# The offsets' convolution in products of one width: 27 products of 32 columns on four strips

## The chip, the cores and the metric

The kernel runs on one core of a Trainium2 chip. The time is that of the device from start to end of the program, in microseconds (us), as the median of several runs. A profile is one execution recorded by the hardware; its span is the time from the first to the last instruction of the program.

## What is computed

The input x is 2 images of 128 channels and 128 x 128 pixels. Two layers are added to it in turn. The first (a gated product with 128 x 128 weights, over group-normalized x) is done before the part that is changed here. The second is a deformable convolution over x after a group norm and a relu: an ordinary 3 x 3 convolution gives 18 offsets per pixel, two for each of nine taps; each tap then samples the image at its own shifted, fractional position, and the nine samples are multiplied by the weights.

```python
x = jax.nn.relu(x)                                   # of the normalized x
offset = conv3x3(x, w_off) + b_off                   # 128 -> 18 channels
py = base_y + off[:, :, 0]                           # off: [image, tap, 2, row, column]
px = base_x + off[:, :, 1]
samp = _bilinear_gather(x, py, px)                   # 128 channels, 9 taps, each pixel
out = jnp.einsum('bckhw,ock->bohw', samp, w_def)     # added to x
```

## The kernel before

All is written out by hand: each engine has its own list of instructions, and semaphores tie them. The first layer fills roughly the first fifth of the span. Then the second runs over 64 bands, each 8 rows by 64 columns of pixels (two sides of 16 row blocks of two images). `bands` (L447) walks a fixed list, `ORDER` (L425), once per band, and each engine does from it the steps that it has. Each step has a lead: in one pass, the offsets of band n + 3 (`O`, `Q`, `h`), the windows `z` of band n + 2, the weights `k` and the transposes `T` of band n + 1, the sampling steps `s0` to `s15` of band n and the nine taps `c0` to `c8` of the last convolution of band n - 1 are done. The part of the list that matters: `h0 s0 s1 s2 k0 h1 c0 c1 s3 s4 T0 k1 z0 z1 O0 s5 s6 P0 k2 c2 c3 s7 s8 T1`.

The pixels that the offsets' convolution reads are split in two float16 numbers. ScalarE makes `z_near` (`cast_z`, L1043: norm and relu from `raw`, a ring of 44 rows; where the rows of a band cross the ring's end this takes two instructions) and casts it to the high part `z_hi` (L1031). VectorE subtracts the two to get the low part `z_lo` (`split_z`, L1392). The weights are split as well: `woff` holds for each tap 32 columns of high part (`woff_hi`) and beside them 32 of low part (`woff_lo`), 18 of each 32 in use.

The step `O0` on TensorE is `offsets` (L901): it waits for `z_hi` and runs `convolve_offset_parts` (L887), which writes one PSUM bank of 128 partitions by 512 pixels. First come nine products of `z_hi`, one for each tap, with the 64 columns of both weight parts, in turn to partitions 0 to 63 and 64 to 127 (L895). Then a wait for `z_lo`, and nine products of `z_lo` with the 32 columns of `woff_hi`, in turn to partitions 64, 0, 96 and 32. What lies in the four strips of 32 partitions is added later, by the `select` matrix. Then ScalarE evicts the bank (`evict_offsets`, L1054).

Around it: ahead of the block TensorE transposes windows (`T0`, L867) and behind it come the sampling matmuls (`s5`, L851), whose results ScalarE (L1070) and VectorE (L1382) copy out of PSUM. GpSimd multiplies the hats into sampling weights, six pieces per band (`weigh`, L1666); the first waits until sampling step 15 of the band before is done. The products of the last convolution are L816, those that place the hats L831 and L834. L765 is a matmul of the first layer.

Of the kernel before, what the change touches and what calls it, by code (L numbers as in the profile page):

```python
# [12 lines left out]
TAPS, NOFF = 9, 18  # L13
# [5 lines left out]
BR, WC, UW = 8, 4, 64  # L19
# [88 lines left out]
def preact_conv_kernel(nc, x, Wa, ba, Wb, bb, Wg, bg, Wo, bo, w_off, b_off, w_def,  # L108
                       ident_d, group_mask_d, select_d, select_all_d, coords_d, out):
    with ExitStack() as ctx:  # L110
        def sb(name, shape, dt=F32):
            return ctx.enter_context(nc.sbuf_tensor(name, shape, dt))
# [15 lines left out]
        bank = [pairs[0][:, 0], pairs[0][:, 1], pairs[1][:, 0], pairs[1][:, 1]]  # L128
# [27 lines left out]
        woff = sb("woff", [P, TAPS, 2 * 32], F16)  # L156
        woff_hi, woff_lo = woff[:, :, 0:32], woff[:, :, 32:2 * 32]
# [56 lines left out]
        z_hi, z_lo = (sb(n, [P, UW + 2, BR + 2], F16) for n in ("z_hi", "z_lo"))  # L214
# [182 lines left out]
        B_OFF, B_CONV, B_ZT, B_S = 0, 2, 3, (4, 5, 6, 7)  # L397
# [286 lines left out]
        def _(pe):  # L684
# [49 lines left out]
            for j in range(3):  # L734
# [6 lines left out]
                             stop=True).then_inc(abg, 1)  # L741
            pe.wait_ge(abg, ABG_STEPS)

            def group(g, s):
# [48 lines left out]
                elif known and g == 6:  # L793
# [11 lines left out]
                             stop=True).then_inc(final, 1)  # L805
            pe.wait_ge(final, 4)
            nc.tensor.matmul(bank[B_ST][:, 2 * GROUPS:3 * GROUPS], average[:], devs2[:],
                             start=True, stop=True).then_inc(final, 1)
# [77 lines left out]

            def convolve_offset_parts(n):  # L887

                products = [(z_hi, k, 2 * 32, k % 2 * 64) for k in range(TAPS)]
                products += [(z_lo, k, 32, (64, 0, 96, 32)[k % 4]) for k in range(TAPS)]  # L890
                for i, (pixels, k, width, at) in enumerate(products):
                    if i == TAPS:
                        pe.wait_ge(z_lo_ready, n + 1)
                    ky, kx = k // 3, k % 3
                    mm = nc.tensor.matmul(  # L895
                        bank[B_OFF][at:at + width, :].rearrange("p (w r) -> p w r", r=BR),
                        woff[:, k, 0:width], pixels[:, kx:kx + UW, ky:ky + BR],
                        start=(i < 2), stop=(i + 4 >= len(products)), tile_position=(0, at))
                return mm

            def offsets(n, u, _):  # L901
                pe.wait_ge(z_hi_ready, n + 1)
                wait(pe, dist_ready, n)
                convolve_offset_parts(n).then_inc(off_done, 1)
# [816 lines left out]
```

## Time and profile before

| | |
|---|---|
| median of 3 runs | 1606.08 us (1605.52 to 1608.66) |
| the profiled execution | 1607.68 us |
| its span | 1605.9 us |
| TensorE busy | 1521.9 us |
| VectorE, ScalarE, GpSimd busy | 1064.8, 1005.7, 909.4 us |
| L895, products of `z_hi`: number, mean | 576, 412 ns |

Busy time is the union of an engine's instructions. Matmuls overlap in the array: a recorded matmul of 512 columns lasts some 380 ns while the next one starts 215 ns after it, so starts say more than durations. PE is TensorE's matmul, PEld its weight load, DVE VectorE, ACT ScalarE, POOL GpSimd. The clock is the share of full speed that was granted.

### The profile page before, as it was taken

Reading aid. Unit: us, or ns where it says so; the run is one execution under the profiler, and the core shown is the slowest. Engines: PE = TensorE matmul, PEld = TensorE weight load, DVE = VectorE, ACT = ScalarE, POOL = GpSimd, SP = SyncE. Lnnn points to the kernel's source line nnn. Section 1 sums busy time; section 2 is a strip of 40 time slices with the busy share of each in tenths; the row PEclk is TensorE's granted clock in tenths of the full one; section 3 lists DMA queues with packets and bytes.
Section 4 is the critical chain, followed back from the end, with each engine's and each line's share of the span. In section 5 each row is a group of like instructions: output and inputs, shape, how many; then the busy total and the mean of one; then the engine's idle time right before and its main releaser. Section 6 shows DMA issues by size and latency. Waiting matters only on the chain.

```text
span 1605.9 us, 27017 instructions
## 1 busy us (share of the span) xinstructions
PE 1521.9 (95%) x8915; PEld 993.1 (62%) x8916; DVE 1064.8 (66%) x2154; ACT 1005.7 (63%) x1820; POOL 909.4 (57%) x563
## 2 busy tenths in 40 slices
PE   5999999955999999999999999999999999999998
PEld 4777777733666566656666666665666665666664
DVE  4888888754566666666666666666666666666664
ACT  2555555535667676667666676666666676666663
POOL 3555555615566566655556666555556665655561
PEclk9999999968999999999999999999999999999999
DMA  4334333335676666666666666666666666666550
GB/s 138 106 115 120 109 110 119 90 115 166 182 214 197 184 195 187 192 189 182 191 189 184 184 189 188 197 193 191 185 185 196 194 192 182 188 193 185 172 161 27
DMA packets 190705, 268.05 MB, mean 167 GB/s; under 512 B 19810, under 2 KB 128382, under 8 KB 190590
## 3 DMA queue, kind: packets, MB, share of 16 engines
q1 hardware_dynamic: 190590, 266.60, 56.7%
q8 instruction: 61, 1.00, 0.3%
q14 instruction: 54, 0.44, 0.1%
HBM read 188.33 MB, written 78.18 MB: 166 GB/s over the span
## 4 chain that ended last, share of the span: by engine, by line
PE 73%; issue 11%; POOL 6%; SPq 3%; DVE 3%; ACT 2%; DMA 1%; POOLq 0%; ACTq 0%; DVEq 0%
PE bank L851 31%; PE pair L816 22%; PE pair L895 7%; PE pair L867 7%; POOL samples_hi L1612 4%; PE pair L831 2%; PE pair L834 2%; DVE z_lo L1392 2%; POOL rstd L1566 1%; DMA hat_x<-hats 1%; POOL samples_lo L1578 1%; ACT samples_hi L1070 1%; ACT abg_space L1043 1%; SPq L622 1%; PE bank L724 1%
## 5 line engine op out<-in xcount | busy, mean ns | idle before, releaser
L1666 POOL TENSOR_TENSOR weights<-hy_all,hx_all 112x768 f32<-112x768 f32 x384 | 723.0, 1918 | 510.6 <-PE bank L851 467.1
L1382 DVE SCALAR_TENSOR_TENSOR samples_lo<-bank,samples_hi 128x288 f16<-128x288 f32 (+1 forms) x1024 | 455.1, 464 | 351.0 <-ACT samples_hi L1070 343.5
L1070 ACT ACTIVATE samples_hi<-bank 128x288 f16<-128x288 f32 (+1 forms) x1024 | 402.2, 420 | 328.9 <-PE bank L851 308.0
L851 PE MATMUL bank<-weights,zT 112*128 112x288 f32 (+1 forms) x2176 | 598.2, 404 | 0.0
L851 PEld LDWEIGHTS bank<-weights,zT 112*128 112x128 f32 x2176 | 381.7, 191 | 131.8 <-issue 36.7
L816 PE MATMUL pair<-samples_hi,w_hi 128*128 128x512 f16 x576 | 219.0, 380 | 1.3 <-DVE samples_lo L1382 1.3
L816 PE MATMUL pair<-samples_lo,w_hi 128*128 128x512 f16 x576 | 217.5, 378 | 0.0
L816 PE MATMUL pair<-samples_hi,w_lo 128*128 128x512 f16 x576 | 217.4, 377 | 0.0
L867 PE MATMUL pair<-ident,z 128*112 128x128 f32 x1088 | 171.7, 273 | 10.4 <-DVE zT L1402 9.0
L867 PEld LDWEIGHTS pair<-ident,z 128*112 128x112 f32 x1088 | 132.4, 133 | 66.4 <-DVE zT L1402 9.9
L972 ACT ACTIVATE samples_hi<-pair,nbias,rstd 128x512 f32<-128x512 f32 x64 | 49.7, 777 | 155.0 <-PE pair L715 94.7
L1578 POOL TENSOR_TENSOR samples_lo<-samples_hi,samples_lo 128x512 f16<-128x512 f32 x64 | 74.1, 1157 | 126.1 <-ACT samples_lo L981 126.0
L1020 ACT ACTIVATE z<-raw,norm_band 128x1904 f32<-128x1904 f32 (+3 forms) x80 | 131.0, 1658 | 0.0
L1080 ACT COPY zT<-pair 112x512 f32<-112x512 f32 (+1 forms) x192 | 91.9, 479 | 37.3 <-PE pair L867 33.2
L1043 ACT ACTIVATE abg_space<-raw,norm_band 128x660 f32<-128x660 f32 (+2 forms) x74 | 104.1, 1420 | 12.2 <-DMA raw<-x_pad 12.2
L895 PE MATMUL pair<-z_hi,woff 128*64 128x512 f16 x576 | 87.3, 412 | 13.0 <-ACT z_hi L1031 13.0
L816 PEld LDWEIGHTS pair<-samples_lo,w_hi 128*128 128x128 f16 x576 | 55.3, 96 | 69.5 <-issue 0.3
L1367 DVE TENSOR_SCALAR hats<-dist 128x1024 f32<-128x1024 f32 x64 | 44.8, 700 | 80.3 <-ACT dist L1063 69.4
L1402 DVE COPY zT<-pair 112x512 f32<-112x512 f32 x128 | 87.8, 686 | 11.7 <-PE pair L867 11.7
L816 PEld LDWEIGHTS pair<-samples_hi,w_lo 128*128 128x128 f16 x576 | 56.5, 98 | 60.3 <-issue 0.3
L816 PEld LDWEIGHTS pair<-samples_hi,w_hi 128*128 128x128 f16 x576 | 55.8, 97 | 59.5 <-DVE samples_lo L1382 17.8
L1063 ACT ACTIVATE dist<-pair 128x1024 f32<-128x1024 f32 x64 | 65.5, 1023 | 37.4 <-PE pair L834 37.4
(141 smaller groups left out, 1762.9 us busy)
## 6 DMA issues: line engine op xcount, KB each, us to landing
hy_all<-hat_y SPq DMA_DIRECT2D x384, 192.0 KB
hx_all<-hat_x SPq DMA_DIRECT2D x384, 192.0 KB
hat_y<-hats SPq DMA_DIRECT2D x256, 126.0 KB
raw<-x_pad SPq DMA_DIRECT2D x68, 272.0 KB, 4.4
x_pad<-hy_all SPq DMA_DIRECT2D x64, 272.0 KB, 3.3
weights<-in_x SPq DMA_DIRECT2D x64, 256.0 KB, 3.0
out<-y SPq DMA_DIRECT2D x32, 512.0 KB, 3.6
hat_x<-hats SPq DMA_DIRECT2D x128, 72.0 KB
```

The costliest lines, as they stand in the source:

```text
L816: mm = nc.tensor.matmul(bank[B_CONV].rearrange("p (h c) -> p h c", h=2), w_part[:, k, :], part[:, u, k::TAPS, k % 3 * HR:k % 3 * HR + HALF ...
L851: mm = nc.tensor.matmul(sampled_step(n, p)[:, :, c0 - first:c1 - first], zT[0:WPIX, u * WINDOWS + w, :], weights[0:WPIX, u, :, c0:c1], sta ...
L867: mm = nc.tensor.transpose(bank[B_ZT][0:WPIX, (w % 4) * P:(w % 4 + 1) * P], z[:, u, w].rearrange("p r c -> p (r c)"), ident[:])
L895: mm = nc.tensor.matmul(bank[B_OFF][at:at + width, :].rearrange("p (w r) -> p w r", r=BR), woff[:, k, 0:width], pixels[:, kx:kx + UW, ky:k ...
L1020: done = nc.scalar.activation(z[:, u, :, rows, :], patches, ACT.Relu, bias=norm_band[:, 1].rearrange("p b n -> p (b n)")[:, n:n + 1], scal ...
L1043: done = nc.scalar.activation(z_near[:, :, r0:r1], raw[:, src:src + r1 - r0, left:left + UW + 2].rearrange("p r w -> p w r"), ACT.Relu, bi ...
L1070: nc.scalar.activation(samples_hi[:, u, :, c0:c1], sampled_step(n, p), ACT.Copy).then_inc(samples_ready, 1)
L1080: nc.scalar.copy(zT[0:WPIX, at:at + c, :].rearrange("p w c -> p (w c)"), bank[B_ZT][0:WPIX, 0:c * P]).then_inc(zT_a, 1)
L1382: nc.vector.scalar_tensor_tensor(out=samples_lo[:, u, :, c0:c1], in0=sampled_step(n, p), scalar=1.0, in1=samples_hi[:, u, :, c0:c1], op0=A ...
L1402: nc.vector.tensor_copy(zT[0:WPIX, at:at + c, :].rearrange("p w c -> p (w c)"), bank[B_ZT][0:WPIX, 0:c * P]).then_inc(zT_v, 1)
L1578: nc.gpsimd.tensor_tensor(xT_lo[:], xT[:], xT_hi[:], ALU.subtract).then_inc(xT_lo_ready, 1)
L1666: nc.gpsimd.tensor_tensor(to, hy_all[0:WPIX, i * TROWS:(i + 1) * TROWS, :], hx_all[0:WPIX, i * TROWS:(i + 1) * TROWS, :], ALU.mult).then_i ...
```

## The change

The offsets' convolution is done as three passes over the nine taps: `z_hi` with `woff_hi`, `z_hi` with `woff_lo`, `z_lo` with `woff_hi`. All 27 products have 32 columns, and product i writes the strip of 32 partitions that begins at 32 (i mod 4). The wait for `z_lo` stands ahead of the nineteenth product instead of the tenth. Nothing else is changed.

```diff
             def convolve_offset_parts(n):
 
-                products = [(z_hi, k, 2 * 32, k % 2 * 64) for k in range(TAPS)]
-                products += [(z_lo, k, 32, (64, 0, 96, 32)[k % 4]) for k in range(TAPS)]
-                for i, (pixels, k, width, at) in enumerate(products):
-                    if i == TAPS:
+                q = 4
+                for i in range(3 * TAPS):
+                    if i == 2 * TAPS:
                         pe.wait_ge(z_lo_ready, n + 1)
+                    k, at = i % TAPS, i % q * 32
+                    pixels, w = ((z_hi, woff_hi), (z_hi, woff_lo), (z_lo, woff_hi))[i // TAPS]
                     ky, kx = k // 3, k % 3
                     mm = nc.tensor.matmul(
-                        bank[B_OFF][at:at + width, :].rearrange("p (w r) -> p w r", r=BR),
-                        woff[:, k, 0:width], pixels[:, kx:kx + UW, ky:ky + BR],
-                        start=(i < 2), stop=(i + 4 >= len(products)), tile_position=(0, at))
+                        bank[B_OFF][at:at + 32, :].rearrange("p (w r) -> p w r", r=BR),
+                        w[:, k, :], pixels[:, kx:kx + UW, ky:ky + BR],
+                        start=(i < q), stop=(i + q >= 3 * TAPS), tile_position=(0, at))
                 return mm
```

## Rows read from the trace of the kernel before

**Rows 1.** The page: engine, busy us, share of the span, number of instructions.

```profile
PE 1521.9 (95%) x8915; PEld 993.1 (62%) x8916; DVE 1064.8 (66%) x2154; ACT 1005.7 (63%) x1820; POOL 909.4 (57%) x563
```

**Rows 2.** Windows: length, busy PE, PEld, DVE, ACT, POOL, clock, DMA share, GB/s.

```profile
750.83:769.72 18.89, 18.89 (x102) 11.61 (x101) 11.98 (x25) 13.13 (x26) 11.35 (x7) 1.00 0.70 200
1092.13:1111.95 19.82, 19.19 (x101) 11.60 (x101) 13.57 (x25) 13.42 (x26) 11.31 (x7) 1.00 0.61 178
```

**Rows 3.** Timeline, an ordinary band: start, us, engine, line, operation, count, idle time before.

```profile
1016.35 1.32 PE L895 MATMUL pair<-z_hi,woff 128*64 128x512 f16 x9
...
1018.41 0.75 PE L851 MATMUL bank<-weights,zT 112*128 112x288 f32 x2
```

**Rows 4.** Waits: engine and line, releaser, us in total, times, longest.

```profile
PEld pair L895 <- DVE z_lo L1392: 17.0, 12, 4.6
```

**Rows 5.** Windows of L895 alone, band 1: length, busy PE, PEld, clock, DMA, GB/s.

```profile
358.00:361.00 3.00, 2.56 (x13) 0.83 (x17) 0.50 0.39 113
```

**Rows 6.** Timeline of PE in narrow windows of the block in rows 3.

```profile
1016.81 0.49 PE L895 MATMUL pair<-z_hi,woff 128*64 128x512 f16 x2
...
1017.08 0.59 PE L895 MATMUL pair<-z_hi,woff 128*64 128x512 f16 x3
...
1017.30 0.38 PE L895 MATMUL pair<-z_hi,woff 128*64 128x512 f16 x1
1017.60 0.45 PE L895 MATMUL pair<-z_lo,woff 128*32 128x512 f16 x4
...
1017.83 0.44 PE L895 MATMUL pair<-z_lo,woff 128*32 128x512 f16 x4
...
1018.10 0.38 PE L895 MATMUL pair<-z_lo,woff 128*32 128x512 f16 x1
```

**Rows 7.** Groups by line, windows holding products 3-5 and 6-8: count, busy, mean ns.

```profile
L895 PE MATMUL pair<-z_hi,woff 128*64 128x512 f16 x3 | 0.7, 432 | 0.0
...
L895 PE MATMUL pair<-z_hi,woff 128*64 128x512 f16 x3 | 0.6, 378 | 0.0
```

**Rows 8.** Timeline of VectorE in the band of rows 3.

```profile
1015.89 0.84 DVE L1392 TENSOR_TENSOR z_lo<-abg_space,z_hi 128x660 f16<-128x660 f32 x1
```

**Rows 9.** Timeline of PE in the first layer.

```profile
201.06 0.83 PE L765 MATMUL pair<-abg_space,samples_lo 128*128 128x128 f16 x12
201.73 0.38 PE L768 MATMUL pair<-samples_lo,abg_space 128*128 128x512 f16 x1
```

**Rows 10.** Timeline of PE in a band that waits for `z_lo`.

```profile
1092.13 1.32 PE L895 MATMUL pair<-z_hi,woff 128*64 128x512 f16 x9
1094.08 0.88 PE L895 MATMUL pair<-z_lo,woff 128*32 128x512 f16 x9 [0.63 <-DVE z_lo L1392]
1094.89 0.51 PE L851 MATMUL bank<-weights,zT 112*128 112x288 f32 x1
```

**Rows 11.** Timeline of ScalarE behind the block in rows 3.

```profile
1021.47 0.90 ACT L1070 ACTIVATE samples_hi<-bank 128x288 f16<-128x288 f32 x2 [1.37 <-PE bank L851]
```

**Rows 12.** Timeline of PEld and PE ahead of the block in rows 3.

```profile
1015.58 0.60 PEld L867 LDWEIGHTS pair<-ident,z 128*112 128x112 f32 x4
...
1015.82 0.60 PE L867 MATMUL pair<-ident,z 128*112 128x128 f32 x4
```

**Rows 13.** Timeline of PEld from 1017.59 to 1017.82.

```profile
1017.60 0.12 PEld L895 LDWEIGHTS pair<-z_lo,woff 128*32 128x32 f16 x8 [0.41 <-issue]
```

**Rows 14.** Timeline of GpSimd, first and third piece; third piece and `z_lo` when waiting.

```profile
1012.41 1.82 POOL L1666 TENSOR_TENSOR weights<-hy_all,hx_all 112x768 f32<-112x768 f32 x1 [7.54 <-PE bank L851]
...
1015.96 2.47 POOL L1666 TENSOR_TENSOR weights<-hy_all,hx_all 112x768 f32<-112x768 f32 x1
...
1091.51 1.82 POOL L1666 TENSOR_TENSOR weights<-hy_all,hx_all 112x768 f32<-112x768 f32 x1
...
1091.68 2.35 DVE L1392 TENSOR_TENSOR z_lo<-abg_space,z_hi 128x660 f16<-128x660 f32 x1
```

**Rows 15.** Timeline of ScalarE, copy of sampling step 15 in the band of rows 3.

```profile
1012.29 0.53 ACT L1070 ACTIVATE samples_hi<-bank 128x432 f16<-128x432 f32 x1 [0.47 <-PE bank L851]
```

## Prediction

> **What bounds the kernel now.** I read the page first, then the kernel band by band, then one band product by product. The page gives TensorE 95% of the span [rows 1]. Windows over whole bands are sharper: an ordinary band lasts 18.89 us and TensorE is busy for all of it, while ScalarE has 13.13, VectorE 11.98 and GpSimd 11.35; a slow band lasts 19.82 with 19.19 of TensorE [rows 2]. So a microsecond taken out of the offsets' convolution (L895) in an ordinary band comes off the span, as long as no other engine turns into the wait.
>
> The block of L895 begins at 1016.35 in the band I chose, and the sampling matmul behind it at 1018.41: 2.06 us [rows 3]. The list of waits says that 12 of the 64 bands wait there for `z_lo` [rows 4]; bands 1 and 2 stand in the opening chain, before the clock has risen for good (0.50 in the stretch of the first of them [rows 5]). That leaves 64 - 12 - 2 = 50 ordinary bands, and the sum is made for these.
>
> **What a product costs.** Narrow windows show single starts. Of the products of 64 columns two run at once: tap 4 starts at 1016.81, tap 6 at 1017.08, tap 8, the ninth, at 1017.30. Of those of 32 columns four start together at 1017.60, four at 1017.83, and the ninth at 1018.10 [rows 6]. Two products on the same columns are thus 0.215 or 0.27 apart, and which of the two it is follows the tap: products 3 to 5 of the nine last 432 ns in the trace and the last three 378 [rows 7], so taps 3 to 5 (those with ky = 1) take 54 ns more than the others. The first product of a strip has its weight load ahead of it: 0.23 to the second. At the end of each half the array runs empty: tap 8 would be done at 1017.30 + 0.215, and the narrow half starts at 1017.60, 0.09 later; behind the last narrow one it is from 1018.10 + 0.215 to 1018.41, again 0.095. Two checks: taps 0 and 2 ahead of tap 4 take 1016.81 - 1016.35 = 0.46, twice 0.215 and a load; and in the narrow half tap 0 and tap 4 ahead of tap 8 take 0.23 + 0.27 = 0.50, the rows' 1018.10 - 1017.60. I use this rule for the change.
>
> **The change, part by part.** *Width.* Nine products of 64 columns, two at a time, become eighteen of 32, four at a time: as much array time, and nine weight loads and nine matmuls more per band. *Strips.* Product i goes to strip i mod 4. Strip 1 has the longest queue, taps 1, 5, 0, 4, 8, 3, 7: its seventh product starts at 0.23 + 0.27 + 0.215 + 0.27 + 0.215 + 0.27 = 1.47 and ends at 1.685. The last product of all, strip 2's seventh, follows it in order and ends with it. *One width.* The emptying in the middle goes, the one at the end stays: 1.685 + 0.095 = 1.78. Half columns that stood idle are filled as well: the ninth wide product ran beside nothing. Against 2.06 this is 0.28 less. *The wait.* It stands at the nineteenth product, which the rule puts at 0.985 after the block's start, 1017.34. `z_lo` is done at 1015.89 + 0.84 = 1016.73 [rows 8], so the wait is met 0.6 us early. Behind it on TensorE queue nine products, the sampling steps 5 and 6 and all that follows. *The extra instructions.* 27 pairs of load and matmul come to 1.47/26 = 56 ns each. L765 has twelve pairs from 201.06 to 201.73, 56 ns each [rows 9], so this pace has been held, for fewer pairs. I take nothing for it. If the narrow half's own pace (0.50/8 = 62 ns) were all that can be held, the block would be 26 x 0.062 + 0.31 = 1.92 and the gain 0.14.
>
> **Where no gain is counted.** In the 12 waiting bands the second half starts when `z_lo` comes (1094.08 in the one shown, 1.95 after its block's start [rows 10]), and nine narrow products come after it as before. Bands 1 and 2 are worth 0 to 0.56 each (the gain at half the clock); I take 0.
>
> **Sum.** 50 x 0.28 = 14.0 us. The span of 1605.9 becomes 1591.9, and the profiled execution, 1607.68 of which 1.8 lies around the span, 1593.7. The median shown, 1606.08, is 1.6 below that execution, so the forecast for the median is **1592**.
>
> **What is late next.** Nothing that I find: behind the block ScalarE, the busiest after TensorE, stands idle for 1.37 us until TensorE's sampling releases it [rows 11], and the 0.28 comes out of that.
>
> **Bounds.** If every product took the longer 0.27, the block would be 0.23 + 6 x 0.27 + 0.095 = 1.945, the gain 0.115 and the sum 5.8: 1600.3. On the other side, 12 waiting bands that gain as well give 3.4, and bands 1 and 2 at most 1.1: 18.5 in all, 1587.6.
>
> **Rivals.** *The wait itself empties the array.* In the rows each emptying has both a new width and a wait, so they don't say which of the two costs the 0.09. If it is the wait, eighteen products end at 0.985 + 0.215 = 1.20, then come 0.095 and the nine with 0.50 + 0.31: 2.105, a loss of 0.045 per band, 2.3 us in all, 1608. Against it: the transposes ahead of the block (L867) have a wait of their own in the code, and yet their first weight load goes at 1015.58, 0.24 before the matmul at 1015.82, which has no idle time ahead of it [rows 12]. The Trainium skill, TensorEngine Tiling (Array Packing), Key Properties, says that a change of the tiling mode, not of the tile, drains the engine; by that rule it is the width alone, and the forecast stands. Chance 0.07.
>
> *Weight loads that don't overlap.* If each round of four paid a load of about 0.095 openly, six rounds behind the first would add 0.57: 2.35 per block, 0.29 more than now, and 50 x 0.29 = 14.5 makes 1620.6. It decides from (2.06 - 1.78)/6 = 0.047 per round. Against it: eight loads of the narrow half go within 0.12 us [rows 13], so half of them while the first four products run, and the second four come 0.23 after the first. The Trainium skill, TensorE: Matmul & The Clock Gate, Part 3, The mechanism, has loads overlap running matmuls only where the row groups differ, and these strips share all rows; here the trace differs from the page. Chance 0.04.
>
> *The slower side that I fear more: `z_lo` comes behind GpSimd's third piece.* In the ordinary band VectorE begins `z_lo` at 1015.89 and GpSimd its third product of hats (L1666) at 1015.96; that piece takes 2.47 us where the first took 1.82. In the waiting band the piece begins at 1091.51 and `z_lo` at 1091.68, and `z_lo` takes 2.35 [rows 14] instead of 0.84. Who comes first decides, and there is 0.07 us to spare. If the edit moved one against the other by that much, the 50 bands would look like the waiting one, 1094.89 - 1092.13 = 2.76 per block: 0.70 more, 35 us, 1641. Against it: both runs of work start from the same event, the end of sampling step 15 on TensorE. GpSimd had been idle for 7.54 us before it [rows 14] and ScalarE, which makes what `z_lo` needs, for 0.47 [rows 15]. The edited block lies behind all of this, and the band before it, shorter by 0.28, moves both starts alike. Chance 0.05.
>
> *Another wait, off the block, takes the whole gain*: 1606. Against it is ScalarE's idle time above. Chance 0.04.
>
> **How the numbers follow.** Forecast, 1589 to 1596: 0.70. The weaker forms (62 ns a pair, or the longer product throughout), 1596 to 1601: 0.10. Emptying at the wait, 1608, and the gain lost, 1606: 0.11. Open loads, 1621, and `z_lo` behind GpSimd, 1641: 0.09. The likeliest is 1592. The range 1587 to 1601.5 takes in the two bounds and leaves out 0.20. About 0.2%, 3.2 us, is what a measurement of this kernel can tell from no change: faster by more 0.80, within it 0.11, slower by more 0.09.
>
> **What would show it.** Right: an ordinary band of 18.6 us; in its block 27 products of one width, four starts at once about every 0.25 us, no empty stretch at the nineteenth, 1.78 to the next sampling matmul; the same 12 bands waiting for `z_lo`, and `z_lo` still at 0.84 elsewhere. Wrong: an empty stretch of 0.1 at the nineteenth (first rival), rounds more than 0.3 apart (second), `z_lo` at 2.35 in ordinary bands (third), or a new wait of TensorE behind the block, at sampling steps 8 to 10 above all (fourth).

## The result

The changed kernel takes **1592.01 us** in the median (1589.83 to 1594.16), beside 1606.24 for the kernel before. The ratio is 0.9918, with a 95% interval of 0.9908 to 0.9928: 0.8% faster. The forecast was 1592, in a range from 1587 to 1601.5.

The line of engines on the page of the changed kernel answers to [rows 1]: 576 more matmuls, and TensorE is busy 14.5 us less.

```profile
PE 1507.4 (95%) x9491; PEld 997.6 (63%) x9492; DVE 1063.6 (67%) x2154; ACT 1006.6 (63%) x1820; POOL 909.2 (57%) x563
```

Windows over whole bands of the changed kernel, each from the start of its block (the products of the offsets' convolution, now L896) to that of the next, columns as in [rows 2]: an ordinary band and one that waits for `z_lo`. The ordinary one has gone from 18.89 to 18.61 and TensorE is still busy for all of it; the waiting one stands at 19.84 (19.82).

```profile
743.36:761.97 18.61, 18.61 (x111) 11.74 (x111) 11.97 (x25) 13.15 (x26) 11.36 (x7) 1.00 0.65 189
1078.58:1098.42 19.84, 19.23 (x110) 11.60 (x109) 13.60 (x25) 13.43 (x26) 11.31 (x7) 1.00 0.61 178
```

The timeline of TensorE in the block of an ordinary band of the changed kernel (start, us, count). From 1003.91 to 1005.69 it is 1.78 us, where [rows 3] had 2.06. No row has idle time, and the first two products of `z_lo` even start before the last two of `z_hi`.

```profile
1003.91 1.15 PE L896 MATMUL pair<-z_hi,woff 128*32 128x512 f16 x16
1004.85 0.38 PE L896 MATMUL pair<-z_lo,woff 128*32 128x512 f16 x2
1004.90 0.38 PE L896 MATMUL pair<-z_hi,woff 128*32 128x512 f16 x2
1005.07 0.70 PE L896 MATMUL pair<-z_lo,woff 128*32 128x512 f16 x7
1005.69 0.75 PE L851 MATMUL bank<-weights,zT 112*128 112x288 f32 x2
```

In the same band `z_lo` is made as before (first row, VectorE), and ScalarE's idle stretch behind the block has shrunk to 1.09 us, from 1.37 in [rows 11] (second row).

```profile
1003.45 0.85 DVE L1393 TENSOR_TENSOR z_lo<-abg_space,z_hi 128x660 f16<-128x660 f32 x1
...
1008.75 0.90 ACT L1071 ACTIVATE samples_hi<-bank 128x288 f16<-128x288 f32 x2 [1.09 <-PE bank L851]
```

Ten bands whose rows cross the end of the ring (ring-end bands below) wait for `z_lo` in both kernels. There the block still takes 2.79 us (1081.37 - 1078.58; [rows 10]: 2.76), with its last nine products held by `z_lo`:

```profile
1078.58 1.37 PE L896 MATMUL pair<-z_hi,woff 128*32 128x512 f16 x18
1080.56 0.88 PE L896 MATMUL pair<-z_lo,woff 128*32 128x512 f16 x9 [0.61 <-DVE z_lo L1393]
1081.37 0.51 PE L851 MATMUL bank<-weights,zT 112*128 112x288 f32 x1
```

**Where the time came from.** One window from the block of band 6 to that of band 63, first of the kernel before, then of the changed one:

```profile
445.98:1531.21 1085.23, 1079.23 (x5701) 661.46 (x5700) 697.87 (x1377) 741.57 (x1393) 646.27 (x343) 1.00 0.65 189
```

```profile
440.69:1512.78 1072.09, 1066.38 (x6214) 667.31 (x6214) 698.20 (x1377) 742.46 (x1393) 646.81 (x343) 1.00 0.66 192
```

That is 13.14 us less. In these 57 bands 9 wait, and 48 x 0.275 = 13.2 (0.275 is the 0.28 with one figure more). The rest of the difference between the two profiles lies ahead of band 6: 2.1 us before the first block, where nothing was changed, and 3.2 in bands 0 to 5, while some 0.5 is lost behind the block of band 63.

The 3.2 are a sum of gains and losses. The gain, 5.9 us, lies between the blocks of bands 3 and 4. TensorE before (first two rows) waits there 3.81 us for a copy of VectorE and then takes 4.53 us for ten sampling matmuls; in the changed kernel (last two rows) it waits 1.23 us and takes 2.37. The granted clock over these matmuls was 0.50 (1.2 GHz) before, from 400.60 to 405.17, and 1.00 (2.4 GHz) after, from 396.75 to 399.11. VectorE had itself waited for a transfer (`hat_x<-hats`), 4.34 us before and 1.46 after.

```profile
400.60 0.46 PE L867 MATMUL pair<-ident,z 128*112 128x128 f32 x1 [3.81 <-DVE zT L1402]
400.85 4.53 PE L851 MATMUL bank<-weights,zT 112*128 112x288 f32 x10
...
396.75 0.32 PE L867 MATMUL pair<-ident,z 128*112 128x128 f32 x1 [1.23 <-DVE zT L1403]
396.90 2.37 PE L851 MATMUL bank<-weights,zT 112*128 112x288 f32 x10
```

Against it, bands 4 and 5, ordinary before (2.06 each), have become slower: their blocks take 2.25 and 2.87 us. In band 5 of the changed kernel GpSimd's piece began 0.04 us ahead of `z_lo`, and the block waited:

```profile
420.48 1.83 POOL L1667 TENSOR_TENSOR weights<-hy_all,hx_all 112x768 f32<-112x768 f32 x1 [0.35 <-DMA hx_all<-hat_x]
...
420.52 2.49 DVE L1393 TENSOR_TENSOR z_lo<-abg_space,z_hi 128x660 f16<-128x660 f32 x1
...
423.06 0.88 PE L896 MATMUL pair<-z_lo,woff 128*32 128x512 f16 x9 [0.70 <-DVE z_lo L1393]
```

Band 3, which waited for `z_lo` before, doesn't any more.

### The profile page after: what moved, and what is told of

Its sections match the earlier page's. It is cut to its first block, busy times and chain, and to the rows that moved or that the text cites. A ratio compares the mean times of both kernels' runs of the same rounds, so it can differ in the third digit from the quotient of the medians.

```text
span 1588.0 us, 28169 instructions
## 1 busy us (share of the span) xinstructions
PE 1507.4 (95%) x9491; PEld 997.6 (63%) x9492; DVE 1063.6 (67%) x2154; ACT 1006.6 (63%) x1820; POOL 909.2 (57%) x563
## 4 chain that ended last, share of the span: by engine, by line
PE 71%; issue 12%; POOL 7%; SPq 3%; DVE 3%; ACT 2%; DMA 1%; POOLq 0%; ACTq 0%; DVEq 0%
PE bank L851 31%; PE pair L816 23%; PE pair L867 7%; PE pair L896 6%; POOL samples_hi L1613 4%; DVE z_lo L1393 2%; PE pair L831 2%; PE pair L834 2%; POOL samples_lo L1579 1%; POOL rstd L1567 1%; ACT samples_hi L1071 1%; ACT abg_space L1044 1%; DMA hat_x<-hats 1%; SPq L622 1%; SPq L611 0%
## 5 line engine op out<-in xcount | busy, mean ns | idle before, releaser
L896 PE MATMUL pair<-z_hi,woff 128*32 128x512 f16 x1152 | 90.4, 410 | 12.7 <-ACT z_hi L1032 12.7
L1403 DVE COPY zT<-pair 112x512 f32<-112x512 f32 x128 | 87.8, 686 | 11.6 <-PE pair L867 11.6
```

The lines of the kernel that those rows point to most:

```text
L896: mm = nc.tensor.matmul(bank[B_OFF][at:at + 32, :].rearrange("p (w r) -> p w r", r=BR), w[:, k, :], pixels[:, kx:kx + UW, ky:ky + BR], sta ...
L1403: nc.vector.tensor_copy(zT[0:WPIX, at:at + c, :].rearrange("p w c -> p (w c)"), bank[B_ZT][0:WPIX, 0:c * P]).then_inc(zT_v, 1)
```

## The experiments

The kernel before ran beside each of these on the same chip (medians 1604.9 to 1605.2); ratios are against it.

**A change of width without a wait, and a wait without a change of width.** Each emptying of the array in the kernel before had both.

```diff
...
+wide = 4
+products = [(z_hi, woff[:, k, :], k, 2, k % 2 * 2) for k in range(wide)]
+narrow = [(z_hi, woff_hi, k) for k in range(wide, TAPS)]
+narrow += [(z_hi, woff_lo, k) for k in range(wide, TAPS)]
+narrow += [(z_lo, woff_hi, k) for k in range(TAPS)]
+products += [(z, w[:, k, :], k, 1, i % 4) for i, (z, w, k) in enumerate(narrow)]
...
```

> The changed kernel, but taps 0 to 3 of the high pixels go as four products of 64 columns (two at a time) and only then nineteen of 32 columns; the result is the same. There is a change of width without a wait (behind the fourth product) and a wait without a change of width (ahead of the fifteenth). Theory (the change of width empties the array): about 0.095 us empty between the fourth and the fifth product, nothing at the fifteenth; the block in an ordinary band 0.51 + 0.095 + 1.25 + 0.095 = 1.95 us against 1.78, so 50 x 0.17 = 8.5 us more, 1600.5. Rival (the wait empties it): no empty stretch behind the fourth, one of 0.095 at the fifteenth.

Measured: 1600.58 us, ratio 0.997 (0.996 to 0.998). First the block's weight loads, then its wide products, their second pair, the matmuls from the first of `z_lo` on and the sampling behind them:

```profile
1010.83 0.14 PEld L899 LDWEIGHTS pair<-z_hi,woff 128*64 128x64 f16 x4 [0.17 <-issue]
1011.44 0.12 PEld L899 LDWEIGHTS pair<-z_hi,woff 128*32 128x32 f16 x8 [0.47 <-issue]
...
1010.84 0.68 PE L899 MATMUL pair<-z_hi,woff 128*64 128x512 f16 x4
...
1011.08 0.43 PE L899 MATMUL pair<-z_hi,woff 128*64 128x512 f16 x2
...
1011.89 0.38 PE L899 MATMUL pair<-z_lo,woff 128*32 128x512 f16 x1
1011.94 0.38 PE L899 MATMUL pair<-z_hi,woff 128*32 128x512 f16 x1
1011.95 0.38 PE L899 MATMUL pair<-z_lo,woff 128*32 128x512 f16 x1
1011.99 0.38 PE L899 MATMUL pair<-z_hi,woff 128*32 128x512 f16 x1
1012.11 0.75 PE L899 MATMUL pair<-z_lo,woff 128*32 128x512 f16 x7
1012.79 0.51 PE L851 MATMUL bank<-weights,zT 112*128 112x288 f32 x1
```

The second pair of wide products starts at 1011.08 (its long tap 3 ends 0.27 later, 1011.35), and the first narrow load goes at 1011.44, 0.09 after that, with no wait there. At the wait the products of `z_lo` come in among those of `z_hi`. The block is 1012.79 - 1010.84 = 1.95 us, as put down, 0.17 more than in the changed kernel. Of that the change of width costs the 0.09; the rest comes, by the sum, from the new start of the narrow products and the other queues of the strips. A wait that is met costs nothing.

**The place of the wait.**

```diff
-if i == 2 * TAPS:
+if i == TAPS:
-((z_hi, woff_hi), (z_hi, woff_lo), (z_lo, woff_hi))[i // TAPS]
+((z_hi, woff_hi), (z_lo, woff_hi), (z_hi, woff_lo))[i // TAPS]
```

> The changed kernel with the passes in the order high pixels by high weights, low pixels by high weights, high pixels by low weights, and the wait for z_lo at the tenth product; 27 products of 32 columns on four strips as before. This is the place of the wait alone. Theory: in ordinary bands z_lo is done some 0.4 us after the block's start and the tenth product's turn is at 0.50, so at most 0.03 is lost (1.78 to 1.81); in the 12 bands that wait, eighteen products instead of nine come after z_lo, 1.29 instead of 0.81, so 0.48 more each: 5.8 us in all, 1598 to 1599. Rival (the wait's place is of no account, the second pass fills the time): 1592.

Measured: 1596.43 us, ratio 0.9945 (0.9932 to 0.9958), 4.4 above the changed kernel. An ordinary block (first two rows, start and end) and a waiting one:

```profile
1007.26 0.67 PE L896 MATMUL pair<-z_hi,woff 128*32 128x512 f16 x8
...
1009.04 0.51 PE L851 MATMUL bank<-weights,zT 112*128 112x288 f32 x1
```

```profile
1081.92 0.88 PE L896 MATMUL pair<-z_hi,woff 128*32 128x512 f16 x9
1083.88 0.67 PE L896 MATMUL pair<-z_lo,woff 128*32 128x512 f16 x8 [1.08 <-DVE z_lo L1393]
...
1085.17 0.51 PE L851 MATMUL bank<-weights,zT 112*128 112x288 f32 x1
```

The ordinary block stays at 1.78; the waiting one goes from 2.79 to 3.25. Ten such bands at 0.46 are 4.6 us, beside 4.4 measured. I had counted twelve, with bands 0 and 3; from the block of band 0 to that of band 6 this profile has 98.85 us and that of the changed kernel 98.62, so nothing like 0.48 for each stands out there. So moving the wait to the nineteenth is worth nothing in ordinary bands and keeps the waiting ones from getting worse.

**The long taps.** The kernel leaves out the middle row of taps: taps 3 to 5 read the pixels of taps 0 to 2.

```diff
-ky, kx = k // 3, k % 3
+ky, kx = (0, 0, 2)[k // 3], k % 3
```

> The changed kernel with the middle row of taps left out of the offsets' convolution: taps 3 to 5 read the pixels of taps 0 to 2 (ky = 0 instead of 1), with their own weights, so the number and form of the products stay. Theory (a product of ky = 1 takes 54 ns more because of where its reads begin): all products 0.215, the block 1.52 + 0.095 = 1.61 us against 1.78, 50 x 0.17 = 8.4 less, and nine faster products in the waiting bands 0.6 less: 1583. Rival (27 pairs of load and matmul can't go faster than the 56 ns each that the changed kernel shows): the block stays at 1.78, 1592.

Measured: 1582.73 us, ratio 0.9864 (0.9847 to 0.988). The groups of L896 in a stretch of the block that holds taps 3 to 5 and others (mean ns), and the block:

```profile
L896 PE MATMUL pair<-z_hi,woff 128*32 128x512 f16 x6 | 0.6, 378 | 0.0
L896 PE MATMUL pair<-z_lo,woff 128*32 128x512 f16 x6 | 0.6, 378 | 0.0
```

```profile
962.87 1.26 PE L896 MATMUL pair<-z_hi,woff 128*32 128x512 f16 x18
963.75 0.81 PE L896 MATMUL pair<-z_lo,woff 128*32 128x512 f16 x9
964.49 0.51 PE L851 MATMUL bank<-weights,zT 112*128 112x288 f32 x1
```

The products last 378 ns there, none 432, and the block is 1.62. The 54 ns go with ky = 1. The 27th product starts 1.31 us after the first, 50 ns for each: the 56 ns of the changed kernel are no limit.

**Another order of the pixels, in two forms.** Both keep the split pixels row by row, and ScalarE writes `z_near` in that order. In the first the results are written with a step of eight, in the second the pixels are read with a step of 66.

```diff
-z_hi, z_lo = (sb(n, [P, UW + 2, BR + 2], F16) for n in ("z_hi", "z_lo"))
+z_hi, z_lo = (sb(n, [P, BR + 2, UW + 2], F16) for n in ("z_hi", "z_lo"))
...
-bank[B_OFF][at:at + 32, :].rearrange("p (w r) -> p w r", r=BR),
-w[:, k, :], pixels[:, kx:kx + UW, ky:ky + BR],
+bank[B_OFF][at:at + 32, :].rearrange("p (w r) -> p r w", r=BR),   # first form
+w[:, k, :], pixels[:, ky:ky + BR, kx:kx + UW],                    # first form
+bank[B_OFF][at:at + 32, :].rearrange("p (w r) -> p w r", r=BR),   # second form
+w[:, k, :], pixels[:, ky:ky + BR, kx:kx + UW].rearrange("p r w -> p w r"),   # second form
...
```

> The changed kernel with the split pixels kept row by row (rows of 66 pixels) instead of column by column (columns of 10), each product reading eight runs of 64 and writing its result with a step of eight; the result is the same. Theory (the 54 ns are paid for each run that begins one element in): an odd start now belongs to kx = 1 and is paid for 8 runs instead of 64, about 0.007 us; the block about 1.63 us, 50 x 0.15 = 7.5 less, 1584.5, if ScalarE writes the new order as fast. Rival (an odd start costs a quarter of the product, however long the runs): taps 1, 4 and 7 take 0.27 and the block stays near 1.78, 1592. Second rival (results written with a step take longer): block over 1.9, 1598 and more.

> The kernel with the split pixels kept row by row, but each product reads them with a step of 66 in the order of the result and writes the result without a step; the result is the same. It tells the step of the writes from that of the reads, since both orders were changed from the first layout. Theory (the writes with a step took the 0.42 us per product): products 0.215 apart, without long ones, the block 1.61 us; z_near takes 0.93 us instead of 1.59 in this layout and no band waits for z_lo, so 50 x 0.17 and 12 less: 1571. Rival (the reads pay as well for a step): products 0.42 apart or more, block 3.1, 1659 or more.

Measured: 1659.07 us, ratio 1.0336 (1.0323 to 1.035), and 1908.17, ratio 1.1884 (1.1865 to 1.1902). The view of L896 in either (duration ns: least, median, most), first form and second:

```profile
L896 PE MATMUL pair<-z_hi,woff x1152: 602/634/1142, 341.5 to 1582.4; 128*32 128x512 f16 x192
```

```profile
L896 PE MATMUL pair<-z_hi,woff x1152: 1087/1215/1274, 342.1 to 1832.2; 128*32 128x512 f16 x192
```

In the first form the block of 27 products takes 3.11 us (1002.31 to 1005.42) and all taps last some 634 ns, but for the first of each strip (602); in the second 7.23 (1179.10 to 1186.33). The first theory of each fell. The first form takes about twice the time per product and the second about five times. The first differs from the changed kernel in its reads too (runs of 64 instead of 8), and the second, which was to tell the two apart, has a step in its reads; that the writes cost the first its time is likely but not shown. Whether the odd start is paid per run can't be seen under that; it stays open. The first form's ScalarE instruction was a find all the same: `z_near` took 0.93 us in the median instead of 1.59, and in neither form does an ordinary or a ring-end band wait for `z_lo`, which fits the next two experiments.

**Who comes first, `z_lo` or GpSimd's third piece.**

```diff
+nc.scalar.activation(sigmoid_of[:], minus_half[:, 0:1], ACT.Copy)
 nc.scalar.activation(z_hi[:], z_near[:], ACT.Copy).then_inc(z_hi_ready, 1)
```

> The changed kernel with one instruction more per band: ScalarE copies one number per partition (about 0.2 us) ahead of the cast to z_hi, so that z_lo begins about 0.2 us later; nothing that it writes is used. Theory (who comes first, VectorE with z_lo or GpSimd with its third piece, decides, and there is 0.07 us to spare): z_lo goes from 0.85 to about 2.3 us in the 50 ordinary bands, ends about 2.1 us after the block's start, the eighteen products of z_hi end at 1.2 and TensorE stands empty until then; the block 2.8 to 3.0 us instead of 1.78, 1.0 to 1.2 more in each, 1642 to 1652. Rival (0.2 us on ScalarE is hidden by its idle time, z_lo has 0.5 us to spare): 1592.

Measured: 1650.55 us, ratio 1.0277 (1.0261 to 1.0294). An ordinary band: ScalarE's extra instruction, VectorE's `z_lo`, GpSimd's third piece, TensorE's block.

```profile
1039.86 0.23 ACT L1032 ACTIVATE sigmoid_of<-minus_half 128x1 f32<-128x1 f32 x1
...
1040.77 2.51 DVE L1394 TENSOR_TENSOR z_lo<-abg_space,z_hi 128x660 f16<-128x660 f32 x1
...
1040.73 1.85 POOL L1668 TENSOR_TENSOR weights<-hy_all,hx_all 112x768 f32<-112x768 f32 x1
...
1041.13 1.37 PE L896 MATMUL pair<-z_hi,woff 128*32 128x512 f16 x18
1043.33 0.88 PE L896 MATMUL pair<-z_lo,woff 128*32 128x512 f16 x9 [0.83 <-DVE z_lo L1394]
1044.14 0.51 PE L851 MATMUL bank<-weights,zT 112*128 112x288 f32 x1
```

The recorded 0.23 us overlap its neighbours, and `z_lo` came only about 0.1 us later against GpSimd. GpSimd's 0.04 us of lead were enough: `z_lo` 2.51 instead of 0.85, the block 3.01 instead of 1.78, 58 us more than the changed kernel in the whole. The rival of the prediction was real, and its price higher than I had put it: against the 2.06 of the kernel before, the block is 0.95 longer, not 0.70, and the whole some 45 us, not 35. In these bands the piece starts 0.40 ahead of the block (1041.13 - 1040.73), in the ring-end band of [rows 14] and [rows 10] 0.62.

**The waiting bands without their cause.** `z_near` of the next band (`H0`, ScalarE's `cast_z`) goes ahead of sampling steps 13 and 14, with and without the edit of this study.

```diff
-"h0 s0 s1 s2 k0 h1 c0 c1 s3 s4 T0 k1 z0 z1 O0 s5 s6 P0 k2 c2 c3 s7 s8 T1 c4 k3 c5 s9 s10 "
-"Q0 k4 c6 G0 T2 s11 s12 c7 k5 T3 s13 s14 c8 T4 s15 R0").split()]
+"s0 s1 s2 k0 h1 c0 c1 s3 s4 T0 k1 z0 z1 O0 s5 s6 P0 k2 c2 c3 s7 s8 T1 c4 k3 c5 s9 s10 "
+"Q0 k4 c6 G0 T2 s11 s12 c7 k5 T3 H0 s13 s14 c8 T4 s15 R0").split()]
...
-ahead = {"c": -1, "s": 0, "k": 1, "T": 1, "z": 2, "h": 3, "O": 3, "P": 3, "Q": 3,
+ahead = {"c": -1, "s": 0, "k": 1, "T": 1, "z": 2, "h": 3, "H": 4, "O": 3, "P": 3, "Q": 3,
...
```

> The changed kernel with z_near of the next band made earlier in ScalarE's list, ahead of the copies of sampling steps 13 and 14 instead of ahead of those of steps 0 to 2; the result is the same. This takes away what makes the 12 bands wait. Theory (those bands wait because their z_near, in two instructions, puts z_lo behind GpSimd's third piece): z_lo then comes in the second piece's time in every band and is done before the nineteenth product's turn; all bands 18.6 us. In the changed kernel a pair of such bands takes 2.4 us more than ordinary ones, and there are five pairs, so 12 us less: 1580. Rival (they wait because ScalarE as a whole is late there, or the copies that z_near now delays hold TensorE up): 1588 or more.

> The kernel before (nine products of 64 columns, nine of 32) with the earlier z_near alone, so that the edit studied here is undone while no band waits for z_lo; the result is the same. Theory (the edit is worth 0.275 us in each band that doesn't wait, and nothing in one that does): the block is 2.06 us in all bands, and this kernel stands 62 x 0.275 = 17 us above the one with the earlier z_near and the edit (1577.9), 1595; against the kernel before it gains the 10 waiting bands' excess only, some 10 us. Rival (the edit takes the same out of the waiting bands, in another place): the distance is 14 as between the kernels before and after, 1592.

Measured: with the edit 1577.85 us, ratio 0.9837 (0.982 to 0.9854), by the ratios 13 us below the changed kernel where 12 were put down; without it 1595.73, ratio 0.9943 (0.9928 to 0.9957). With the edit, two ring-end bands and, in the first of them, GpSimd's second piece and `z_lo`:

```profile
1072.82:1091.43 18.61, 18.61 (x111) 11.78 (x111) 12.34 (x25) 13.39 (x26) 11.33 (x7) 1.00 0.63 190
1091.43:1110.04 18.61, 18.61 (x111) 11.80 (x111) 12.34 (x25) 13.43 (x26) 11.32 (x7) 1.00 0.67 195
```

```profile
1070.64 1.82 POOL L1667 TENSOR_TENSOR weights<-hy_all,hx_all 112x768 f32<-112x768 f32 x1
...
1071.78 1.39 DVE L1393 TENSOR_TENSOR z_lo<-abg_space,z_hi 128x660 f16<-128x660 f32 x1
```

In every band behind the opening `z_lo` now waits for the second piece; here it ends at 1073.17, in time for the nineteenth product. The ring-end bands have become ordinary. The distance between the two kernels is 17.9 us (17.0 by the ratios), against 17 put down and 14 for the rival. From the block of band 6 to that of band 63, first without the edit and then with it:

```profile
445.59:1522.13 1076.54, 1076.54 (x5701) 665.54 (x5700) 703.80 (x1377) 755.69 (x1393) 644.58 (x343) 1.00 0.65 190
```

```profile
440.07:1500.84 1060.77, 1060.77 (x6214) 672.45 (x6213) 703.92 (x1377) 755.66 (x1393) 645.00 (x343) 1.00 0.66 194
```

That is 15.77 us less, 57 bands at 0.277, with TensorE busy throughout: where no band waits, the edit is worth its 0.28 in all.

**Taps in another order.** This edit is made to the changed kernel with the earlier `z_near`.

```diff
-k, at = i % TAPS, i % q * 32
+k, at = (0, 1, 2, 6, 7, 3, 4, 5, 8)[i % TAPS], i % q * 32
```

> The kernel with the earlier z_near, and the taps of each pass in the order 0, 1, 2, 6, 7, 3, 4, 5, 8; the result is the same. Theory (a strip's time is the sum of its products, 0.27 for taps 3 to 5 and 0.215 for the others): no strip has more than two of the long ones behind its first product and seven in all, the block ends 0.054 earlier, 1.73 us; 64 x 0.054 = 3.4 us less than the kernel with the earlier z_near, 1576.5. Rival (27 products share a pace and the order is of no account): as that kernel, 1580.

Measured: 1577.99 us, ratio 0.9826 (0.9811 to 0.9841). An ordinary block:

```profile
1073.95 1.32 PE L896 MATMUL pair<-z_hi,woff 128*32 128x512 f16 x18
1074.94 0.81 PE L896 MATMUL pair<-z_lo,woff 128*32 128x512 f16 x9
1075.69 0.51 PE L851 MATMUL bank<-weights,zT 112*128 112x288 f32 x1
```

1.74 us instead of 1.78, and a band of 18.56 instead of 18.61: the rule for a strip's time holds here too. In the median of the whole the 3 us can't be told from none; the intervals of the two kernels overlap. In the profiles, from the block of band 6 to that of band 63, it is 1058.11 us beside 1060.77. Of the versions tried, these two are the fastest.

## Why the prediction was right

- **The bound.** TensorE filled the ordinary band before and after. What left its block left the band: 0.28 of 0.28 (18.89 to 18.61), and ScalarE's idle stretch behind the block paid, as put down.
- **The cost of a product.** 0.215 or 0.27 by tap, 0.095 at a change of width: the block came out at 1.78, the number of the sum. The missing middle row (1.62 for 1.61) and the other order of taps (1.74 for 1.73) confirm the first, the width without a wait confirms the second. Of the 0.28, the 0.09 of the emptying was measured alone; the rest, the idle half columns beside the ninth wide product and the better filled strips, is shown only by the sums' meeting these blocks.
- **One step was wrong and did no harm.** I let products start in the order of issue across strips, which puts the nineteenth at 0.985. It started at 0.94 (1004.85), ahead of the seventeenth and eighteenth at 1004.90. Here strips don't wait for each other; the end is set by the longest strip's own queue, which I had summed.
- **The wait.** Met in time in the ordinary bands, free of cost there. The first rival (the wait empties the array) fell by the rows of the block, and by the experiment on the width.
- **The extra pairs.** Nothing, as taken; the weaker form (62 ns a pair) and the open loads fell with the block's 1.78.
- **The waiting bands.** No gain in the ten ring-end bands, 2.79 to 2.76, and removing their cause showed the gain appear in them. The sign "the same 12 bands waiting" didn't hold: the other two were bands 0 and 3 before and are bands 0 and 5 in the changed kernel's profile.
- **`z_lo` and GpSimd.** From band 6 on they stayed apart by their 0.07 us in the ordinary bands; both start from sampling step 15, and the edit lies elsewhere. In band 5 the order did turn, as the third rival feared for all. There the piece came from a DMA wait, not from step 15. That the order hangs on so little is shown by the extra instruction as well.
- **The opening.** I took bands 1 and 2 as 0 and had bands 4 and 5 among the ordinary, 0.56 in all; these two lost instead, 0.19 and 0.81 in their blocks. The two profiles still differ by 3.2 us in the opening, through the shorter wait and the higher clock between bands 3 and 4, which the sum didn't have. The pair with the earlier `z_near` differs there by 4.0 (101.6 and 97.5 us from band 0 to band 6). That the edit brings this about is not shown: the kernel with the extra instruction has the edit too, and there the ten sampling matmuls took 4.53 us as before.
- **The number.** That the median came out within 0.1 us of the forecast is luck: the runs of either kernel spread over more than 4 us, the ratio gives 13.2 us with 11.6 to 14.8, and the sum had two bands too many among the ordinary and nothing for the opening. What the prediction can claim is the 0.28 per ordinary band and the bands in which it doesn't show.

## What to carry to other kernels

Where products run side by side on column strips of the array, sum each strip's own queue from single starts in the trace, and look for the time lost at every change of strip width; a whole block in one width can be cheaper with half as many instructions again. Before counting on it, list the bands in which the engine isn't the bound, and give the gain to the others alone. And look for pairs of instructions on VectorE and GpSimd that begin within a tenth of a microsecond of each other: an edit far smaller than this one can turn their order.

## What the runs showed of the hardware

- A product of 512 columns whose runs of eight begin one element in (ky = 1) lasted 432 ns, 54 longer than the others; with its reads moved to those of ky = 0 it lasted 378.
- A change of strip width emptied the array for about 0.09 us; a wait already met, within one width, cost nothing.
- On four strips at once, 512 columns took 0.215 us with reads in runs of eight and writes in order, 0.42 with reads in runs of 64 and writes at a step of eight, and about 1.0 with reads at a step of 66 and writes in order.
- Strips started their products out of the order of issue, by 0.05 us here.
- Ten sampling matmuls took 4.53 us at a granted clock of 0.50 (1.2 GHz), right after TensorE had stood idle for 3.81 us, and 2.37 at 1.00 (2.4 GHz), after 1.23 us idle.
- ScalarE's 128 x 660 took 1.59 us when it had to turn rows into columns and 0.93 when it didn't.
- 0.04 us decided whether a subtraction on VectorE took 0.85 or 2.51 us beside a product on GpSimd. The Trainium skill, SBUF — State Buffer, SBUF: two separate sides, says that a VectorE instruction with two SBUF inputs and a GpSimd one that reads SBUF exclude each other for a whole instruction, and that the first to start blocks the other; both the 2.51 of VectorE and GpSimd's 2.47 in [rows 14] agree.
